# One full transpose turns the router's scores back, GpSimd joins expert pieces, SyncE holds the last output waits

## The reference

```python
# state-space layer, on n = layernorm(x)
s = sigmoid(silu(n @ s_w1.T + s_b1) @ s_w2.T + s_b2)
u = (n @ B_w.T + B_b) * s
h_t = h_(t-1) @ A.T + u_t              # scan over the 4096 rows, 128 states
y = h @ C_w.T + C_b + n @ D_w.T + D_b
x = x + y * sigmoid(n @ g_w.T + g_b)
# expert layer, on m = layernorm(x)
scores = m @ gate_w.T                  # 8 scores a row
chosen = argmax(scores)
x = x + m + m @ expert_w[chosen].T     # m + ... per row, one expert each
```

## Time and profile before

| | |
|---|---|
| runs shown | 916.02 to 917.07 us, median of 3: 916.51 us |
| the profiled execution | 915.37 us, of which the profile's span is 913.6 us |
| TensorE busy (matmuls) | 894.5 us (98%) |
| TensorE weight loads | 722.8 us (79%), beside the matmuls |
| VectorE busy | 674.2 us (74%) |
| ScalarE busy | 651.8 us (71%) |
| GpSimd busy | 403.2 us (44%) |

### The profile page before, as it was taken

How to read it: one execution, slowest core, us unless ns; L and a number is a source line. 1 busy time by engine, 2 the same in 40 slices (tenths; PEclk the granted TensorE clock), 3 DMA queues, 4 the chain that set the end, 5 groups by cost and what they waited for, 6 DMA issues and landing times. The chain is left out here.

```text
span 913.6 us, 15779 instructions
## 1 busy us (share of the span) xinstructions
PE 894.5 (98%) x4461; PEld 722.8 (79%) x4462; DVE 674.2 (74%) x1697; ACT 651.8 (71%) x878; POOL 403.2 (44%) x640
## 2 busy tenths in 40 slices
PE   8999999999999999999999999999999999999995
PEld 7777878787878878787878878787877887888884
DVE  6777878788887878788787888787786465555552
ACT  5578697978879797978879797978534445666661
POOL 1033536281735536181735537181523453443442
PEclk9999999999999999999999999999999999999998
DMA  8445395867768495867668495867889879988871
GB/s 315 132 92 142 90 220 127 200 149 190 153 165 205 96 218 131 198 149 192 154 159 208 98 215 136 199 144 174 296 273 413 340 249 252 217 221 211 199 188 37
DMA packets 231049, 172.36 MB, mean 189 GB/s; under 512 B 155701, under 2 KB 189237, under 8 KB 229952
## 3 DMA queue, kind: packets, MB, share of 16 engines
q1 hardware_dynamic: 220032, 137.71, 60.5%
q0 software_dynamic: 10800, 33.70, 11.0%
q10 hardware_dynamic: 144, 0.07, 0.0%
HBM read 81.63 MB, written 54.68 MB: 149 GB/s over the span
## 5 line engine op out<-in xcount | busy, mean ns | idle before, releaser
L1757 PE MATMUL y<-experts,x1T_hi 128*128 x568 | 180.5, 399 | 0.8 <-DVE x1T_lo L1402 0.8
L597 POOL TENSOR_SCALAR ln_var_eps<-ln_mean_var 128x4 f32<-128x4 f32 x16 | 3.6, 224 | 277.0 <-DVE ln_mean_var L1078 276.9
L652 POOL DMA_INDIRECT out<-gate,ids x71 | 72.6, 1022 | 111.1 <-DVE gate L1421 78.6
L1757 PEld LDWEIGHTS y<-experts,x1T_hi 128*128 128x128 f32 x568 | 103.2, 188 | 20.8 <-issue 1.1
L1757 PE MATMUL y<-experts,x1T_lo 128*128 x284 | 111.5, 392 | 0.0
L587 POOL TENSOR_TENSOR y_biased<-y_biased,gate 128x256 f32<-128x256 f32 x120 | 93.3, 799 | 25.6 <-DVE y_biased L1068 25.5
L1456 PE MATMUL gates<-GwT_hi,xT_hi 128*128 128x512 f32 x256 | 104.0, 406 | 0.0
L1456 PE MATMUL y<-DwT_hi,xT_hi 128*128 128x512 f32 x256 | 102.6, 401 | 0.5 <-DVE gateT L1000 0.5
L1458 PE MATMUL gates<-GwT_hi,xT_lo 128*128 128x512 f32 x256 | 100.5, 393 | 0.0
L1421 DVE TENSOR_TENSOR gate<-y,raw_weights 128x512 f32<-128x512 f32 x71 | 49.0, 691 | 69.4 <-PE y L1757 63.8
L1457 PE MATMUL gates<-GwT_lo,xT_hi 128*128 128x512 f32 x256 | 100.2, 391 | 0.0
(11 more groups left out here) (283 smaller groups left out, 2328.9 us busy)
## 6 DMA issues: line engine op xcount, KB each, us to landing
raw_weights<-routed_rows SPq DMA_DIRECT2D x71, 258.0 KB, 3.2
x_in<-L_attn_x SPq DMA_DIRECT2D x32, 512.0 KB, 4.2
x_rows<-L_attn_x SPq DMA_DIRECT2D x32, 512.0 KB, 5.1
turned_experts<-raw_weights SPq DMA_DIRECT2D x32, 512.0 KB, 3.6
experts<-turned_experts SPq DMA_DIRECT2D x8, 2048.0 KB, 14.6
raw_weights<-L_ffn_expert_w SPq DMA_DIRECT2D x32, 256.0 KB, 3.1
routed_rows<-padrow SPq DMA_DIRECT2D x9, 258.0 KB, 4.6
out<-gate,ids POOLq DMA_INDIRECT x71, 3.9
```

Source lines behind the costliest of these rows:

```text
L652: nc.gpsimd.indirect_dma_start(out=out_rows, out_offset=bass.IndirectOffsetOnAxis(ap=ids[r][:, 0:1], axis=0), in_=res[r], in_offset=None, ...
L1757: ins = nc.tensor.matmul(Y[m % 2][:], x2T[a][:, k, m % 2 * P:(m % 2 + 1) * P], flat[:, bass.ds(first + (w * KD + k) * D, D)], start=(k == ...
```

## The change

The change has three parts.

1. `scT` becomes a tile of 128 partitions by 128, zeroed once by GpSimd's memset. `scoresT` copies each tile's 16 rows of 128 values to partitions of their own (0, 32, 64, 96), so one copy of 256 columns becomes two of 128. `tail_back(b)` is one transpose of 128 by 128, in the place of the second of before, and the first is gone; `choose` reads the scores from their new places. Since `scT` is read once for all four tiles, the second pair's first product now waits for the copy of the first pair (`scoresT_ready`).
2. In blocks 1 to 14 the join of both pieces is made by GpSimd, as a `tensor_copy` of the same values, behind `add_identity` and ahead of `rstd2`. ScalarE keeps the joins of blocks 0 and 15.
3. The four waits for `out_sent` at the end go from GpSimd's stream to SyncE's.

```diff
-    SC_RANK, SC_COUNT, SC_TURN = 2 * NT * E, 3 * NT * E, 2 * P
+    QUAD = P // NT
+    SC_RANK, SC_COUNT, SC_TURN = P, P + NT * E, 2 * P
...
-        scT = kb("scoresT", [2 * E, 2 * P])
+        scT = kb("scoresT", [P, P])
...
             for d in (SLOTS - 4, SLOTS - 2):
                 flip_odd(d % M, d // M)
+            for r in range(R):
+                sp.wait_ge(out_sent[r], 16 * len(range(r, SLOTS, R)))
...
+            def join_piece(b, j):
+
+                pool.wait_ge(w_flip[j], 16 * (b + 1))
+                pool.wait_ge(w_low[j], b)
+                nc.gpsimd.tensor_copy(planes(w_whole[j].rearrange("p k t -> p (k t)")),
+                                      w_flipped[j].rearrange("p (h k) t -> p h (k t)", h=2)).then_inc(w_joined[j], 1)
...
                 if 0 < b < LASTB:
                     for j in range(2):
                         add_identity(b + 1, j)
+                if 0 < b < LASTB:
+                    for j in range(2):
+                        join_piece(b, j)
                 if b > 0:
                     rstd2(b - 1, 1 - q)
...
             slot_store(SLOTS - 1, (SLOTS - 1) % R)
-            for r in range(R):
-                pool.wait_ge(out_sent[r], 16 * len(range(r, SLOTS, R)))
...
-                nc.scalar.activation(scT[:], score_bank(b)[0:2 * E, SC_TURN:], ACT.Copy).then_inc(S_["scoresT_ready"], 1)
+                for i in range(2):
+                    at = (2 * pair + i) * QUAD
+                    ins = nc.scalar.activation(scT[at:at + 2 * E, :], score_bank(b)[0:2 * E, SC_TURN + i * P:SC_TURN + (i + 1) * P],
+                                               ACT.Copy)
+                ins.then_inc(S_["scoresT_ready"], 1)
...
-                act.wait_ge(w_flip[j], 16 * (b + 1))
-                wait(act, w_low[j], b)
-                nc.scalar.activation(planes(w_whole[j].rearrange("p k t -> p (k t)")),
-                                     w_flipped[j].rearrange("p (h k) t -> p h (k t)", h=2), ACT.Copy
-                                     ).then_inc(w_joined[j], 1)
+                if b in (0, LASTB):
+                    act.wait_ge(w_flip[j], 16 * (b + 1))
+                    wait(act, w_low[j], b)
+                    nc.scalar.activation(planes(w_whole[j].rearrange("p k t -> p (k t)")),
+                                         w_flipped[j].rearrange("p (h k) t -> p h (k t)", h=2), ACT.Copy
+                                         ).then_inc(w_joined[j], 1)
...
-                dve.wait_ge(S_["scores_psum"], 2 * b + 2)
+                dve.wait_ge(S_["scores_psum"], b + 1)
...
                     pe.wait_ge(S_["x2T_lo"], NT * b + 2 * pair + 2)
+                    if pair > 0:
+                        counted_waits(pe, (S_["scoresT_ready"], 2 * b + pair))
...
-            def tail_back(b, pair):
-
-                counted_waits(pe, (S_["scoresT_ready"], 2 * b + pair + 1))
-                for i in range(2):
-                    at = (2 * pair + i) * 2 * E
-                    ins = nc.tensor.transpose(score_bank(b)[:, at:at + 2 * E], scT[:, i * P:(i + 1) * P], ident[0:2 * E, 0:2 * E])
-                ins.then_inc(S_["scores_psum"], 1)
+            def tail_back(b):
+
+                counted_waits(pe, (S_["scoresT_ready"], 2 * b + 2))
+                nc.tensor.transpose(score_bank(b)[:, 0:P], scT[:], ident[:]).then_inc(S_["scores_psum"], 1)
```

More of the change, by code:

```diff
@@ L549, in _ @@
                     nc.gpsimd.memset(xrow[0][:, :, D:RW], 0.0), nc.gpsimd.memset(xrow[1][:, :, D:RW], 0.0),
-                    nc.gpsimd.memset(zeros[:], 0.0), nc.gpsimd.memset(onehot[:, NT, :], 0.0), nc.gpsimd.memset(taken[:], 0.0)]
+                    nc.gpsimd.memset(zeros[:], 0.0), nc.gpsimd.memset(scT[:], 0.0), nc.gpsimd.memset(onehot[:, NT, :], 0.0), nc.gpsimd.memset(taken[:], 0.0)]
             for ins in made:
@@ L1088, in choose @@
             def choose(b):
-                dve.wait_ge(S_["scores_psum"], 2 * b + 2)
-                nc.vector.tensor_reduce(scores[:], score_bank(b)[:, 0:SC_RANK].rearrange("p (t h e) -> p t e h", h=2, e=E),
+                dve.wait_ge(S_["scores_psum"], b + 1)
+                parts = score_bank(b)[:, 0:SC_RANK].rearrange("p (t q) -> p t q", q=QUAD)[:, :, 0:2 * E]
+                nc.vector.tensor_reduce(scores[:], parts.rearrange("p t (h e) -> p t e h", e=E),
                                         AX.X, ALU.add).then_inc(S_["scores_ready"], 1)
@@ L1695, in body @@
                 gates(b, 1, 0, 1)
-                if tail:
-                    tail_back(b - 1, 0)
                 if not by_dma(b - 1, NT - 1):
@@ L1706, in body @@
                     if tail:
-                        tail_back(b - 1, 1)
+                        tail_back(b - 1)
                     over(b, 5)
@@ L1785, in last_tail @@
                     tail_scores(LASTB, 0)
-                elif s == 10:
-                    tail_back(LASTB, 0)
                 elif s == 11:
@@ L1790, in last_tail @@
                 elif s == 13:
-                    tail_back(LASTB, 1)
+                    tail_back(LASTB)
                 elif s == 15:
```

## The result

The changed kernel takes 948.3 us (median of 4 runs, 943.1 to 949.9) where the kernel before takes 916.3 us; the ratio is 1.034, with a 95% interval of 1.031 to 1.037. The forecast was 912.5 us with a range up to 923.5. It is slower by 32 us, and outside the range. The sign is that of rival 1, the size is nobody's.

The account below looks back on a forecast made before the run. TensorE's instruction order was taken to bound the steady blocks. Per block -0.44 - 0.23 + 0.5 = -0.17, times 13 = -2.2, then -0.2, -0.5 and -1.35: -4.2 us from 916.51, giving 912.5 us, range 907.5 to 923.5.

Parts of the forecast that it names:

- rival 1: GpSimd's first copy starts before VectorE's cast of 124 columns, making TensorE's gates late: +0.6 a block, 922.3 us; chance 0.28.
- The deciding term: GpSimd's copies hold up VectorE's scan subtraction, so TensorE's gates start late: +0.5 us per steady block.
- The transposes: On TensorE, removing the first pair saves 0.26 alone, up to 0.44; one full transpose for the second saves 0.23.
- SyncE's waits: At the kernel's end, GpSimd's drain can start earlier without the output waits: 1.35 us saved.
- Rival 2: No hold-up from GpSimd's copies reaches TensorE: -0.49 a block, period 40.5 us, total 908.1 us; chance 0.17.
- If the cast goes first, only the subtraction is held: VectorE's cast precedes GpSimd's first copy; the subtraction waits until about 290.08, TensorE's gates start 0.4 late: +0.5 a block.
- The cast is held to 289.95: With GpSimd's first copy ahead, VectorE's cast waits for it alone, the subtraction for the second; TensorE 1.17 + 0.1 late.
- The length of a copy: GpSimd's join copy of 1024 columns was taken as 1.05 us, from the rate at which GpSimd writes.
- late weights: Behind TensorE's late gates, the weights come late as well, costing another 0.1 us.
- So this just about fits: At the block's end ScalarE comes 0.07 later, TensorE 0.23 earlier; cost nothing, up to 0.1 a block.
- Block 15 and the slots: Outside the steady blocks, the transpose edits save 0.2 us in block 15 and 0.5 in the slots.
- longer copies under rival 1 are left out: The range stopped at 923.5, though GpSimd copies of 1.5 us would cost another 6 us or more.

Follow-up runs that it names:

- sp: The kernel before with only the last output waits moved from GpSimd to SyncE: 914.4 us (0.9979).
- best: high with one join a block on GpSimd behind VectorE's split of 124 columns, and the identity additions behind that of 120: 907.8 us (0.990).
- gaps: The changed kernel with GpSimd's first join waiting for VectorE's split of 124 columns, the second for that of 120: 919.9 us (1.0036).
- pause: The changed kernel with only GpSimd's second join waiting, until VectorE has split the states of 124 columns: 922.4 us (1.0078).
- joinonly: The kernel before with only the joins of blocks 1 to 14 moved to GpSimd: 941.5 us (1.028).
- filled: The changed kernel with eight unneeded 512-column matmuls ahead of the waiting scan step in blocks 2 to 14: 942.5 us (1.029).
- nojoin: The changed kernel with all joins back on ScalarE; the full transpose and SyncE's waits stay: 915.5 us (0.9988).
- high: nojoin with ScalarE's split of the next block's tile 1 moved ahead of its wait for the scores: 911.9 us (0.9957).
- apart: high with GpSimd's identity additions waiting until VectorE has split the states of 124 columns: 911.8 us (0.9965).

## Why the prediction was wrong

**What it had right.** The deciding term was named as such: GpSimd's copies against VectorE's cast and subtraction of 124 columns, with TensorE's gates behind them and a margin of 0.28 us. The transposes came out as costed (0.28 against 0.26 for the first pair, 0.27 against 0.23 for the second, entry after 0.23). SyncE's waits were worth 1.4 against 1.35 by the drain's rows (sp as a whole gained 2.1 us by the medians, with an interval of 0.5 to 3.2). Rival 2's 40.5 us a block is what best reaches, but only with ScalarE's split moved and one join a block left on ScalarE; with the copies alone moved, in gaps, a block takes 41.3 or more. The terms add up to 912.3 us, not 912.5, which changes nothing.

**Who goes first.** The step that failed is "If the cast goes first, only the subtraction is held", and with it rival 1's "The cast is held to 289.95". Both let VectorE's next instruction in whenever one GpSimd instruction ends. pause and the changed kernel show that this cast doesn't come in between additions and copies that follow each other without a pause. So the cast could not go first, since the identity additions stood right ahead of the copies. It was held to the end of both copies, 2.4 us in block 6 and 2.8 in block 7 (where it starts at 344.63, during the additions), where the forecast had 0 and rival 1 0.9. The alternation that the prediction assumed does occur, in the very rows it read it from. Behind the pair of the earlier trace rows GpSimd's next pair follows without a pause:

```profile
112.82 1.89 POOL L587 TENSOR_TENSOR y_biased<-y_biased,gate 128x256 f32<-128x256 f32 x2
```

VectorE's subtraction of 512 columns ends at 113.42. At its usual 0.68 it ran from about 112.74, so it did come in behind the pair that ended at 112.87, and it was GpSimd that waited: 1.89 us for two where 1.45 is usual. The same is seen in every run of this case. What the prediction did was to carry this over to another operation beside other GpSimd work, where it doesn't hold. Why the subtraction of 512 columns gets its turn and the split of 124 columns does not was not tested. The earlier trace rows settle nothing: the subtraction there is held, yet it ends at 287.81, before the addition starts at 287.83.

**The length of a copy.** 1.34 us, not 1.05. The writing rate of a memset was the wrong row to stand next to; the rows of operations that read gave 1.5 to 1.6, and the answer lies nearer to them. With two copies held in full this is 0.6 us a block.

**What a wait of TensorE costs behind it.** 0.1 us was put down for late weights. Wherever the step comes late, the drift grows by 0.38 on the step and the gates behind it, in joinonly in every block.

**The clock.** It was not in the sum. The longer waits of the changed kernel were followed by a fall in seven of eight blocks, the shorter ones in one of five, and a fall cost 1.4 to 1.8 us, nearly as much again as the wait. At least 10 of the 38 us of the steady blocks, by filled, are this.

**The block's end.** "So this just about fits" failed: the two copies cost ScalarE 0.17, not 0.07, and TensorE, 0.5 us early, waits 0.31 there. With what follows it that is 0.4 of the 0.55 us that the transposes saved. The late steps of nojoin cost some 5 us more over the thirteen blocks (eight at 41.2 to 41.7 against 40.83), and the whole transpose part is worth nothing against sp (915.5 and 914.4), where -0.26 - 0.23 a block was expected. The first half of this is shown, the cause of the late steps is not.

**Elsewhere.** Block 15 and the slots had -0.7. What follows block 14 got 3.9 us shorter in the changed kernel, 1.8 in nojoin and 2.2 in sp, where the drain's 1.4 is the only edit. One execution of each can't tell the 0.7 from such scatter.

**The range.** Rival 1, with copies longer than it assumed, was left out at the top ("longer copies under rival 1 are left out"). Its own text priced 1.5 us copies at 6 us more or beyond, and that tail should have been inside. Even so it ends near 928 us, 20 short of the result: the queue and the clock are what was missing.

**Left open.** VectorE's first addition to the states of 124 columns starts in some blocks 0.3 to 1.2 us after TensorE's step has ended, with nothing in the trace between them, and with or without GpSimd beside it (high, block 10: the step ends at 451.62, the addition starts at 452.53). In the profiled executions this is so in no block of the kernel before, four of sp, eight of nojoin, three of high, two of apart, four of best and five of the changed kernel, and without a held cast it makes the step of 120 columns late. The blocks of sp have the order of before, so no edit in a block is needed for it. Why it is rarer in high than in nojoin was not settled either: the medians say that the edit helps, and one trace of each can't say how.

## What to carry to other kernels

Before an operation is moved to GpSimd, list what VectorE does in that stretch, and let the copy wait for the end of VectorE's chain, not stand behind other GpSimd work: here one wait (pause) was worth 26 us and two (gaps) 28, with the same instructions. Price a hold at one instruction and also at everything that GpSimd has ready in a row, since both occur here. And if TensorE's gap grows towards the 1.8 us seen here, price the clock behind it from rows, and look for the next engine whose chain has no pause, since an edit that speeds up TensorE alone stops there.

## What the runs showed of the hardware

- VectorE's cast of 124 columns (SBUF to SBUF) waited 2.4 us through two GpSimd copies of 1.34 us, and 1.59 us (pause) through the rest of an addition and one copy; it came in between two that stood back to back in no steady block of the changed kernel, joinonly and filled. A VectorE subtraction of 512 columns (1.16 us in place of 0.68) did come in between two back-to-back pairs of GpSimd's operations, of which the second took 1.89 us in place of 1.45. An addition of PSUM and SBUF ran through at 0.30.
- A GpSimd addition queued behind an indirect DMA went with a VectorE subtraction held while the DMA instruction still ran (0.65 us). With no addition queued it was 0.30 in all nine such blocks of apart, and it was also 0.29 in three blocks of the changed kernel with the addition queued.
- TensorE's granted clock was 0.50 behind an idle time of 1.84 us (block 7) and 1.00 behind one of 1.42 us (block 6), with one exception on either side among the thirteen blocks, and stayed at 1.00 when the idle time was filled with matmuls. It also stayed at 1.00 behind 2.13 us of idle time in block 2 of joinonly.
- GpSimd's drain ended 6.20 us after the end of its last instruction (941.6 to 947.8) in the changed kernel, and 6.20 us after its last wait (907.2 to 913.4) in the kernel before.
